# A decoder layer on one core: cross-attention's maxima transposed in mid-step, attended values copied ahead of the first exponential and formed ahead of the last score

## What is computed

```python
x = _layernorm(x + self_attention(x, Wq, Wk, Wv, Wo))      # 16 heads, rotary, causal
x = _layernorm(x + _L0_xattn_ref(x, ctx, ctx, gamma))      # the change is in here
x = _layernorm(x + ffn(x))                                  # 1.58-bit linear layers

def _L0_xattn_ref(q, k, v, gamma):      # q, k, v: (32, 128, 512)
    B, Dq, Lq = q.shape                  # the middle axis, 128, is split over 8 heads of 16
    qh = q.reshape(B, 8, 16, Lq); kh = k.reshape(B, 8, 16, 512); vh = v.reshape(B, 8, 16, 512)
    qk = einsum('bhdq,bhdl->bhql', qh, kh) / sqrt(16)       # 512 x 512 scores for each head
    sm = softmax(qk, axis=-1)
    return gamma * einsum('bhql,bhdl->bhdq', sm, vh).reshape(B, 128, Lq)
```

## Time and profile before

| what | value |
|---|---|
| three timed runs | 1809.01, 1811.45, 1829.64 us; median 1811.45 us |
| the profiled execution | 1802.17 us, of which the span is 1800.3 us |
| TensorE, matmuls | 1611.2 us busy, 90% of the span |
| VectorE | 1521.2 us, 84% |
| ScalarE | 1328.8 us, 74% |
| GpSimd | 1092.0 us, 61% |
| mean granted TensorE clock | 0.945 |

### The profile page before, as it was taken

One profiled execution on the slowest core, in us unless ns is written; L12 is line 12 of the kernel. 1 busy time (PEld: TensorE's weight loads), 2 busy tenths in 40 slices (PEclk: granted clock), 3 DMA queues, 4 the chain that ended last, 5 costly groups with the idle time before them and its releaser, 6 DMA issues. The chain is left out here.

```text
span 1800.3 us, 35221 instructions
## 1 busy us (share of the span) xinstructions
PE 1611.2 (90%) x12000; PEld 873.2 (49%) x12000; DVE 1521.2 (84%) x1894; ACT 1328.8 (74%) x2821; POOL 1092.0 (61%) x1532
## 2 busy tenths in 40 slices
PE   6999999999998798999999999999867877778764
PEld 5777777777776333333333333333323333333332
DVE  5778787888787897999999999999568898988885
ACT  4666555454545387888888888888778888888993
POOL 6667676766766442355553555423467888888872
PEclk9999999999998798999999999999978888888897
DMA  4455434343446454444555554445333333333311
GB/s 144 144 177 175 136 107 135 106 130 117 120 126 169 117 99 114 120 109 120 125 158 156 160 131 116 111 120 127 94 114 91 113 104 116 106 106 112 106 53 41
DMA packets 119269, 217.10 MB, mean 121 GB/s; under 512 B 32241, under 2 KB 34705, under 8 KB 116785
## 3 DMA queue, kind: packets, MB, share of 16 engines
q1 hardware_dynamic: 110770, 213.64, 41.7%
q0 software_dynamic: 8320, 1.21, 0.4%
HBM read 137.67 MB, written 76.02 MB: 119 GB/s over the span
## 5 line engine op out<-in xcount | busy, mean ns | idle before, releaser
L969 DVE TENSOR_REDUCE b_smax<-wide 128x2 f32<-128x1024 f32 x512 | 620.6, 1224 | 46.3 <-PE wide L1029 33.4
L945 ACT ACTIVATE b_prob<-bank 128x512 f32<-128x512 f32 x1024 | 555.9, 599 | 96.7 <-PE bank L1077 90.8
L1077 PE MATMUL bank<-b_xs,b_cs 50*128 50x512 f32 x1024 | 327.6, 476 | 12.4 <-DMA b_xs<-b_max_part 11.4
L1059 PE MATMUL sums<-b_prob,b_vT 128*32 128x256 f32 (+1 forms) x3584 | 316.0, 424 | 5.6 <-ACT b_prob L945 0.5
L1029 PE MATMUL wide<-b_cs,b_xs 48*128 48x512 f32 x1024 | 280.9, 435 | 8.8 <-DVE b_smax L969 7.3
L1077 PEld LDWEIGHTS bank<-b_xs,b_cs 50*128 50x128 f32 x1024 | 132.9, 186 | 220.0 <-ACT b_prob L945 167.8
L885 POOL TENSOR_SCALAR b_max_part<-b_neg_max 16x128 fp32r<-16x128 f32 x64 | 18.4, 288 | 303.1 <-ACT b_neg_max L936 302.4
L370 ACT ACTIVATE a_prob<-wide,a_neg_max 128x128 f32<-128x128 f32 x512 | 181.5, 418 | 2.5 <-DVE a_neg_max L461 2.5
L1987 PE MATMUL wide<-c_w,c_xqT 128*128 128x512 bf16 x512 | 166.5, 498 | 0.0
L895 POOL DMA_DIRECT2D b_xs<-b_max_part x256 | 133.6, 527 | 42.1 <-POOL b_max_part L888 37.3
L1059 PEld LDWEIGHTS sums<-b_prob,b_vT 128*32 128x32 f32 x3584 | 72.7, 108 | 163.3 <-issue 96.9
(11 more groups left out here) (156 smaller groups left out, 3351.6 us busy)
## 6 DMA issues: line engine op xcount, KB each, us to landing
scratch_c_part<-a_c_part SPq DMA_DIRECT2D x64, 256.0 KB
scratch_x_part<-a_x_part SPq DMA_DIRECT2D x64, 256.0 KB
b_xs<-scratch_x_part SPq DMA_DIRECT2D x128, 128.0 KB, 3.1
b_cs<-scratch_c_part SPq DMA_DIRECT2D x128, 128.0 KB, 3.1
scratch_heads<-b_heads SPq DMA_DIRECT2D x64, 256.0 KB, 2.9
a_xT<-in_xT SPq DMA_DIRECT2D x32, 256.0 KB, 6.4
a_c_in<-in_ctx SPq DMA_DIRECT2D x32, 256.0 KB, 2.6
a_x<-in_x SPq DMA_DIRECT2D x32, 256.0 KB, 4.2
```

The costliest lines, as they stand in the source:

```text
L945: act.activation(prob[k % 8][:, :], e_ps[bank_of(UNITS * t + k)][:, :], ACT.Exp, scale=0.25).then_inc(exp_done, 1)
L969: dve.tensor_reduce(smax[g][:, :, j, qc], m_ps[u % 2][:, :, :], AX.X, ALU.max, negate=True).then_inc(max_done, 1)
L1059: last = pe.matmul(av_ps[2 * XD * h:2 * XD * (h + 1), cols], vT[p][:, lc, XG * g + h, :], prob[(XG * n + 2 * j + e) % 8][:, cols], start=( ...
L1077: pe.matmul(e_ps[bank_of(UNITS * t + 2 * u + e)][:, :], cs[p][g][half(e), j, lc * P:(lc + 1) * P], xs[p][g][half(e), j, :], start=True, st ...
```

## The change

Three edits, all in cross-attention.

1. TensorE's step: the transposition of the maxima moves from the end of steps 0 and 4 to behind product part 0, the middle of the step; it waits for one max unit less (it no longer needs VectorE to be through with the next batch's unit in `m_ps[0]`) and writes to `m_ps[1]`. So the max unit that must wait for the copy of the transposed maxima is now unit 1 (and 9), which stands directly behind half 0 of score pair 2n+1 in the same step.
2. TensorE's step: in steps 1 and 5 product part 1 (512 columns there) stands ahead of half 1 of score pair 2n+1, which was ahead of it.
3. ScalarE's step: the copy of the heads moves ahead of the first exponential of steps 1 and 5, and the copy of the maxima moves from behind the fourth exponential of steps 0 and 4 to behind the second.

```diff
@@ evict_max, transpose_max: both use m_ps[1] in place of m_ps[0]
-            act.activation(neg_max[g][:, :], m_ps[0][0:XG * KC, 0, 0:P], ACT.Copy).then_inc(neg_done, 1)
+            act.activation(neg_max[g][:, :], m_ps[1][0:XG * KC, 0, 0:P], ACT.Copy).then_inc(neg_done, 1)
@@ scalar: step
                 for j in range(XG):
                     k = XG * n + j
+                    if j == 0 and n == 1 and not first:
+                        copy_heads(t - 1, 1, first=second)
+                    if j == 0 and n == 5:
+                        copy_heads(t, 0, first=first)
                     act.wait_ge(score_done[k % 2], PAIRS * t + k // 2 + 1)
...
-                    if j == 0 and n == 1 and not first:
-                        copy_heads(t - 1, 1, first=second)
-                    if j == 0 and n == 5:
-                        copy_heads(t, 0, first=first)
-                if n == 0:
-                    evict_max(t, 1, first=first)
-                if n == 4 and not last:
-                    evict_max(t + 1, 0)
+                    if j == 1 and n == 0:
+                        evict_max(t, 1, first=first)
+                    if j == 1 and n == 4 and not last:
+                        evict_max(t + 1, 0)
@@ tensor: step
             for n in range(STEPS):
                 score(s, p, 2 * n, (0, 1), first)
-                for j in range(2):
-                    if not last:
-                        u = 2 * n + j
-                        max_unit(*after(s, p), u, after_mt={2: 2 * t + 2, 10: 2 * t + 3}.get(u))
-                    if j == 0:
-                        attended(n, 0)
-                    score(s, p, 2 * n + 1, (j,), first)
-                attended(n, 1)
+                if not last:
+                    max_unit(*after(s, p), 2 * n)
+                attended(n, 0)
+
                 if n == 0:
-                    transpose_max(s, p, 1, PAIRS * (t + 1) + (0 if last else 1))
+                    transpose_max(s, p, 1, PAIRS * (t + 1))
                 if n == 4 and not last:
-                    transpose_max(*after(s, p), 0, PAIRS * (t + 1) + 9)
+                    transpose_max(*after(s, p), 0, PAIRS * (t + 1) + 8)
+                score(s, p, 2 * n + 1, (0,), first)
+                if not last:
+                    max_unit(*after(s, p), 2 * n + 1, after_mt={1: 2 * t + 2, 9: 2 * t + 3}.get(2 * n + 1))
+                if n % KC == 1:
+                    attended(n, 1)
+                score(s, p, 2 * n + 1, (1,), first)
+                if n % KC != 1:
+                    attended(n, 1)
```

More of the change, by code:

```diff
@@ L1035, in transpose_max @@
             pe.wait_ge(max_done, beside)
-            pe.transpose(m_ps[0][0:XG * KC, 0, 0:P], smax[g][:, :, :, :].rearrange("p e b c -> p (e b c)"),
+            pe.transpose(m_ps[1][0:XG * KC, 0, 0:P], smax[g][:, :, :, :].rearrange("p e b c -> p (e b c)"),
                          ident[:, :]).then_inc(mt_done, 1)
@@ L1112, in begin @@
             while u < to:
-                max_unit(0, 0, u, first=True, after_mt=1 if u == 10 else None)
-                if u == 9:
-                    transpose_max(0, 0, 0, 9)
+                max_unit(0, 0, u, first=True, after_mt=1 if u == 9 else None)
+                if u == 8:
+                    transpose_max(0, 0, 0, 8)
                 u += 1
```

## The result

The changed kernel takes 1871.6 us (median of four executions, 1850.9 to 1873.0) where the one before takes 1814.8. The ratio is 1.0285, 95% interval [1.0235, 1.0334]: slower by 2.9%. (1814.8 us is the median of four executions, one more than the three whose median of 1811.45 us the prediction counted from.) The profiled execution has a span of 1871.0 us, 70.7 more than before. The median lies 20 us above the upper end of the range that was given, 1802 to 1852 us.

The account below looks back on a forecast made before the run. TensorE's matmul starts bound cross-attention; steps 0 to 2 sum to 8.40 us against 7.93, +0.47 for each of 61 transpositions, 29 us, less 4 for DMAs: 1811.5 + 25 = 1836.5 us, range 1802 to 1852.

Parts of the forecast that it names:

- What bounds the kernel: Cross-attention: TensorE's loop of four score and max matmuls in two slots, then a product, repeating at 1.24 us.
- Step 0: Cross-attention step with the moved transposition: forecast 3.18 us against 2.48 for a plain step, +0.70.
- Transposition to max unit: In step 0, the max unit waits for the copy of the maxima and starts 0.73 us behind the transposition.
- Step 1: Up to the moved score: the wait for the heads' copy goes, 2.13 us where it took 2.76, -0.63.
- Moved score to the product of step 2: Step 2's product part 0 waits for exponential 7: 0.54 + 0.60 + 0.14 = 1.28 us behind the moved score, +0.61.
- Step 2: Cross-attention step that takes in the moved score: forecast 3.09 us, +0.61 from waiting for exponential 7.
- The sum for a transposition: Steps 0 to 2 of cross-attention: 8.40 us against 7.93, +0.47 for each of 61 transpositions, 29 us.
- The DMA credit: Maxima leave 1.24 us earlier in their step, so scores wait less for their DMAs: at most 7 us, taken as 4.
- The clock: Rival: new TensorE gaps of 0.3 to 0.6 us bring half clock, time past 2000 us; chance 0.02.
- this slot: In step 2, the lone score's extra TensorE slot of 0.23 us, by the array-packing rule without the wait for exponential 7.

Follow-up runs that it names:

- e11: Changed kernel with GpSimd's stores of the feed-forward weights' sums moved from cross-attention into self-attention; median 1855.2 us over twelve executions.
- e7: Changed kernel with both product parts of steps 3 and 7 joined behind the last score, the dense form; 1839.6 us, ratio 1.0124 to the kernel before.
- e10: Changed kernel with steps 3 and 7 lengthened by a wait of the last score, matmul order unchanged; 1876.2 us, ratio 1.0334 to the kernel before.
- e8: Kernel before with GpSimd's stores of the weights' sums moved into self-attention, behind its step 16; 1808.9 us against 1815.7, ratio 0.9964.

## Why the prediction was wrong

By its own steps:

- **What bounds the kernel**: right. TensorE's start-to-start distances gave every full-clock duration to a few hundredths.
- **Step 0**, forecast 3.18 us: 3.21 (1055.93 to 1059.14). Transposition to max unit, forecast 0.73: 0.73.
- **Step 1** up to the moved score, forecast 2.13: 2.12 (1059.14 to 1061.26). The wait for the copy of the heads is gone, as said.
- **Moved score to the product of step 2**, forecast 1.28: 1.18, and the wait named there, for exponential 7, is in the row at 1062.44. Exponential 7 starts at 1061.79 and takes 0.60, so the signal takes 0.05 us here and not the 0.14 that was read off two other places. Step 2 is 2.99 instead of 3.09.
- **The sum for a transposition**, forecast +0.47: +0.39. 61 of them forecast 29 us: 24.
- **The DMA credit**, 4 us: 4.4 us. Some luck is in that: the longest of these waits, at the start of batch 3, lies between 2.3 and 5.8 us in the nine kernels whose profiled executions have it.
- **The clock** is the step that failed: the sum had no term for it. It stood as a rival with a chance of 0.02, weighed by whether gaps of 0.3 to 0.6 us would bring the clock down. They don't: in the changed kernel no stretch at half clock begins at one of them. But the kernel before already had 34 us at half clock in these two stretches, the first row lies in one of them, and the prediction didn't ask what ends such a stretch. The change lengthened both, 34 to 140 us in the profiled executions, and that is 43 of the 70.7 us. The rival's price was wrong too: it took half clock to be for good and the time past 2000 us. And that the clock stayed at 1.00 around a wait of 1.1 us held for that wait, not as a rule: five waits of 0.8 to 1.5 us in other kernels had a fall with them.

The prediction weighed what the Trainium skill states in "TensorEngine Tiling (Array Packing)", Key Properties: different tiles of the array can work in parallel. The trace agrees. Three scores on two halves take 0.73 us from start to end at 1061.26, where a pair takes 0.50; and what step 2 loses to this slot is covered by the longer chain through ScalarE (1.18 us against the 0.90 of the prediction's layout).

Not every execution of the changed kernel is slow for this reason. e11 is the changed kernel less the trigger, which was worth 7 us to the kernel before (1815.7 against 1808.9), and had executions of 1818 us; so the order can give about 1825 by this estimate, near the 1827 us that the sum gave for a good execution. The four executions measured have mean clocks of 0.914 to 0.928, and the one with a trace has both long stretches.

## What to carry to other kernels

Where a row of the granted clock falls below full anywhere in a stage, ask of a change not only whether its gaps could bring the clock down, but what the engine was doing each time the clock came back, and whether the change leaves that in place. A form of the loop that costs nearly the same at full clock (0.13 us a step in e7) can make the recovery much likelier. Look upstream as well: find what made the engine wait long enough to lose the clock (here 256 words stored one by one) and move that. It gave the kernel before 0.4%, but it didn't cure the changed one, which has a second stretch with another start (e11).

## What the runs showed of the hardware

- A TensorE that the trace has as busy for 99% of 128 us was at 1.2 GHz throughout (e10). In e7 the clock rose 1.7 to 2.1 us into the step behind the first dense one in all three cases.
- TensorE's waits of 2.3 to 5.8 us had a fall of the clock from 1.00 to 0.50 with them in nine of nine profiled executions, waits of 0.7 to 1.7 us in 5 of 22 cases.
- A batch of cross-attention takes 36.2 us at half clock and 21.6 us at full clock, 1.7 times as long and not twice.
- The length of a stretch at half clock differs from execution to execution of one kernel: the mean clock of e11's twelve executions spans 0.905 to 0.946, its times 73 us.
- Two DMAs that store 128 single words each, issued at 664.8 us, stand ahead of a time in which the maxima's DMA of the kernel before took up to 9.9 us to land, against a median of 2.1. With the stores moved away (e8) the longest landing is 5.4 us, and the wait is gone. From the views of line 895 before and of the same line, 898, in e8:

```profile
DMA to landing us min/median/max: 1.6/2.1/9.9
...
DMA to landing us min/median/max: 1.5/2.0/5.4
```
